# Loading the slot registers of the message sums one tile ahead of the row registers, on TensorE

## The chip, the core and the metric

The kernel runs on one core of a Trainium2 chip. The metric is the device time of one execution in microseconds, as the median of several runs. Engines are named as in the profile: PE is TensorE's matmuls, PEld its weight loads, DVE the vector engine, ACT the scalar engine, POOL is GpSimd, SP issues DMAs. A "q" behind an engine's name (PEldq) marks its sequencer, which runs register operations and waits.

## What is computed

The reference is a graph network of four layers, each followed by a residual and a layer norm. The change touches the fourth, an edge-conditioned convolution that repeats six steps over 212,500 edges of 12,500 nodes, with 32 features:

```python
eh = relu(e_feat @ en1_w.T + en1_b)
w_e = (eh @ en2_w.T + en2_b).reshape(-1, D, D)      # a 32 x 32 matrix for each edge
for _ in range(STEPS):                               # 6
    msg = einsum('ei,eio->eo', out[src], w_e)        # a message for each edge
    agg = segment_sum(msg, dst, num_segments=n_nodes) + conv_bias
    h = _gru_cell(relu(agg), h, ...)
    out = h
```

## The kernel before

Edges are sorted by destination. 128 edges are a tile, 16 tiles a group; a step has 104 groups (TG), and 110 (PG) groups of sums, since edges that don't fit spill into a tail. The edge matrices are not kept: each step computes them anew, tile by tile, in a loop on five engines whose turns two groups make (buffers s = 0 and 1).

For tile j of group g, the engines do this:
- GpSimd gathers the rows of the source nodes by an indirect DMA (line 1957), eight tiles ahead (LEAD), and multiplies the last 320 of 1024 products (`times`, line 1966).
- TensorE computes the 1024 entries of each edge's matrix (`matrices`, line 2066: two matmuls of 512 columns, four passes in the trace) into one of two buffers `p_w`. It first waits on `used`, which DVE raises when it has read the buffer two tiles earlier.
- ACT copies the 320 last entries out for GpSimd (`copy`, line 2010), and prepares the one-hot matrices `apart` for the sums.
- DVE multiplies the first 704 entries with the gathered rows (line 2147), then reduces the products of two tiles earlier (line 2136); for this it waits on `pooled`, GpSimd's part of that tile. Once per group it adds a finished sum (line 2118).
- TensorE sums messages by destination (`sum_up`, line 2082) with a small matmul. Where the sum goes (`row_regs`) and which slot of the ring of messages it reads (`slot_regs`) are registers: 16 of each, one per tile of the group.

The sums lag the matrices by eight tiles (LATER). Each turn j of `group` on TensorE issues the matrices of tile j and then one sum: for j below 8 one of the last eight sums of the group two back, from j = 8 on one of the first eight sums of the group before. At the first sum of a group `sum_up` loads both sets of registers from `slot_d` and `window_d` and then waits for the messages, for the one-hot matrices and for a cleared accumulator. All engines take their instructions in the order in which they are written; the order on TensorE is written out by hand.

Of the kernel before, what the change touches and what calls it, by code (L numbers as in the profile page):

```python
# [33 lines left out]
G = 16  # L34
# [7 lines left out]
TG = -(-E // (P * G))  # L42
# [15 lines left out]
def build(nc, a, out):  # L58
# [6 lines left out]
    class Phase(ExitStack):  # L65
# [6 lines left out]
        def sb(self, name, shape, dt=F32):  # L72
            return self.enter_context(nc.sbuf_tensor(f"{self.tag}_{name}", shape, dt))
# [37 lines left out]
    with top:  # L111
# [24 lines left out]
        with Phase('const') as ph:  # L136
# [3 lines left out]
            with nc.Block() as block:  # L140
                @block.sync
                def _(sp):
                    sp.dma_start(X[:, :], nodes(a["x"]).rearrange("l b f -> l (b f)")).then_inc(x_in, 16)
                    sp.dma_start(table[:, :], a["x"][:, :]).then_inc(x_in, 16)

                    sp.dma_start(wide_table[N:N + 1, :],
                                 a["zeros"][0:1, 0:2 * D]).then_inc(x_in, 16)
                    sp.wait_ge(x_in, 48)
                    sp.wait_ge(made, 4)
                    for i in range(4):  # L150
                        for j in range(4):
                            sp.dma_start(same_f[i * D:(i + 1) * D, j * D:(j + 1) * D],
                                         ident[0:D, 0:D]).then_inc(done, 16)
                    sp.wait_ge(done, 16 * 16)
# [398 lines left out]
        slot_regs = [nc.tensor.alloc_register(f"slot_at{j}") for j in range(G)]  # L553
        ring_regs = [nc.scalar.alloc_register(f"ring_at{s}") for s in range(2)]
        slot_d = sb("slot_d", [1, PAIRS], I32)
# [58 lines left out]
        with Phase("weights") as ph:  # L614
            zeroed, w_in = ph.sem("zeroed"), ph.sem("w_in")
            with nc.Block() as block:
                @block.vector
                def _(dve):
                    for t, _ in weights:
                        dve.memset(t[:, :], 0.0).then_inc(zeroed, 1)  # L620

                @block.sync
                def _(sp):
                    n = 0
                    for k, (_, parts) in enumerate(weights):
                        sp.wait_ge(zeroed, k + 1)
                        for to, of in parts:
                            with nc.allow_non_contiguous_dma(reason="bias columns"):
                                sp.dma_start(to, of).then_inc(w_in, 16)
                            n += 1  # L630
                    sp.wait_ge(w_in, 16 * n)
            ph.end()
# [1240 lines left out]
        with nc.Fori(0, STEPS) as step:  # L1873


            with Phase("l3m") as ph:
# [22 lines left out]
                LATE, LATER = 2, 8  # L1899
# [12 lines left out]
                with nc.Block() as block:  # L1912
# [146 lines left out]
                    @block.tensor  # L2059
                    def _(pe):  # L2060
                        def matrices(i, s, j):
                            t = (i * 2 + s) * G + j

                            pe.wait_ge(used, t + 1)
                            for c in range(2):
                                ins = pe.matmul(p_w[j % 2][:, c * 512:(c + 1) * 512], hid[s][:, j * P:(j + 1) * P],  # L2066
                                                en2[:, c * 512:(c + 1) * 512], start=True, stop=True)
                            ins.then_inc(mats, 1)

                        def sum_up(i, s, j, tail=False):  # L2070
                            g = i * 2 + s
                            if j == 0:
                                pe.load(slot_regs, slot_d[0:1, bass.ds(g * G, G)])
                                pe.load(row_regs, window_d[0:1, bass.ds(g * G, G)])
                                pe.wait_ge(found if tail else hits, g * 4 + 4)

                                pe.wait_ge(joined, (TG * PARTS if tail else g * PARTS + PARTS) + JOINED)

                                pe.wait_ge(cleared, g + 1)
                            at = pe.snap(row_regs[j], min_val=0, max_val=(G - 1) * D)  # L2080
                            of = pe.snap(slot_regs[j], min_val=0, max_val=(RB * G - 1) * D)
                            pe.matmul(p_sum[s][0:LO, bass.ds(at, D)], apart[s][:, j, :], slots[:, bass.ds(of, D)],  # L2082
                                      start=False, stop=True, skip_group_check=True).then_inc(summed, 1)

                        def group(i, s, older=True, newer=True):
                            pe.wait_ge(hid_in[s], i * 16 + 16)
                            for j in range(G):
                                matrices(i, s, j)
                                if j >= LATER:
                                    if newer:  # L2090
                                        sum_up(i + (s - 1), 1 - s, j - LATER)
                                elif older:
                                    sum_up(i - 1, s, G - LATER + j)

                        pe.sem_inc(summed, SUMMED)
                        pe.sem_inc(mats, MATS)
                        group(0, 0, older=False, newer=False)
                        group(0, 1, older=False)
                        with pe.Fori(1, TG // 2) as i:
                            group(i, 0)  # L2100
                            group(i, 1)
                        for j in range(G - LATER, G):
                            sum_up(TG // 2 - 1, 0, j)
                        for j in range(G):
                            sum_up(TG // 2 - 1, 1, j)
                        with pe.Fori(TG // 2, PG // 2) as i:
                            for s in range(2):
                                for j in range(G):
                                    sum_up(i, s, j, tail=True)
# [225 lines left out]
```

## Time and profile before

| | |
|---|---|
| time, median of 3 runs | 36760.22 us (36759.47 to 36788.16) |
| the profiled execution's own time | 36759.45 us |
| its span, from the first to the last instruction | 36757.7 us |
| PE busy | 27737.6 us (75%) |
| DVE busy | 25860.5 us (70%) |
| ACT busy | 12358.7 us (34%) |
| POOL busy | 28300.5 us (77%) |

The message loop fills the last 58% of the span, in six equal steps with a short stage for the node states between them. The shares are means over the whole span, and within the loop three engines are busy most of the time. What the loop waits for is therefore read from idle times and from the distance between equal instructions, not from shares.

### The profile page before, as it was taken

What the parts mean: (1) busy time and instruction counts of PE and PEld (TensorE: products, weight loads), DVE (VectorE), ACT (ScalarE), POOL (GpSimd) and SP (SyncE); (2) the same over time, 40 slices, a digit from 0 to 9 for tenths busy, and PEclk for the clock granted to TensorE, in tenths of its full rate; (3) what the DMA queues carried; (4) which work ended last, traced back from release to release, by engine and by line L of the source; (5) the groups of instructions that cost most, each with busy time, mean ns of one, the idle gap of its engine ahead of it and who ended that gap; (6) DMA issues with size and microseconds to landing.
All of it is one profiled execution on the core that took longest, in us unless ns stands there. A gap on an engine that the chain in (4) does not pass through costs nothing. (4 is left out here: it accounts for less than half of the span.)

```text
span 36757.7 us, 442832 instructions
## 1 busy us (share of the span) xinstructions
PE 27737.6 (75%) x91956; PEld 15930.9 (43%) x91957; DVE 25860.5 (70%) x34107; ACT 12358.7 (34%) x38546; POOL 28300.5 (77%) x30158
## 2 busy tenths in 40 slices
PE   6333346655583333499999999999999999999999
PEld 5000014445583333344444444444444444444444
DVE  8444432222451121399999999999999999999998
ACT  0000001111200000155555555555555555555554
POOL 1776777767507767699979997999799979988997
PEclk8555556655655555599999999999999999999999
DMA  0221012221310000111111111111111111111111
GB/s 19 48 47 29 23 39 82 81 33 27 84 41 14 14 14 14 23 49 49 49 45 49 49 49 45 49 49 49 45 49 49 49 45 49 49 45 48 49 49 44
DMA packets 1452401, 1590.59 MB, mean 43 GB/s; under 512 B 953756, under 2 KB 1115535, under 8 KB 1346959
## 3 DMA queue, kind: packets, MB, share of 16 engines
q1 hardware_dynamic: 743720, 1056.16, 9.1%
q0 software_dynamic: 645120, 473.02, 7.4%
q10 hardware_dynamic: 63360, 59.50, 0.6%
q14 instruction: 169, 1.38, 0.0%
q8 instruction: 32, 0.52, 0.0%
HBM read 1342.34 MB, written 246.33 MB: 43 GB/s over the span
## 5 line engine op out<-in xcount | busy, mean ns | idle before, releaser
L2066 PE MATMUL l3m_p_w<-en,l3m_hid 128*128 128x512 f32 x39936 | 19534.1, 617 | 177.2 <-DVE l3m_prod L2147 101.1
L2136 DVE TENSOR_REDUCE l3m_xg<-l3m_prod 128x32 f32<-128x1056 f32 x9984 | 12423.2, 1244 | 0.3
L1957 POOL DMA_INDIRECT l3m_xg<-wide_table,l3m_mt x9984 | 9783.8, 980 | 2452.9 <-issue 1549.9
L2147 DVE TENSOR_TENSOR l3m_prod<-l3m_p_w,l3m_xg 128x704 f32<-128x704 f32 x9984 | 8827.0, 884 | 542.0 <-ACT l3m_rest L2010 541.9
L1966 POOL TENSOR_TENSOR l3m_prod<-l3m_rest,l3m_xg 128x320 f32<-128x320 f32 x9984 | 8741.6, 876 | 366.6 <-ACT l3m_rest L2010 192.5
L2066 PEld LDWEIGHTS l3m_p_w<-en,l3m_hid 128*128 128x128 f32 x39936 | 6785.0, 189 | 5141.0 <-issue 4795.3
L2010 ACT COPY l3m_rest<-l3m_p_w 128x320 f32<-128x320 f32 x9984 | 4254.7, 426 | 9434.1 <-PE l3m_p_w L2066 8033.8
L2082 PEld LDWEIGHTS l3m_p_sum<-room,l3m_apart 128*125 128x125 f32 x21120 | 3936.3, 197 | 5586.1 <-issue 5586.1
L1996 ACT ACTIVATE l3m_apart<-iota_lo,l3m_lo 128x125 f32<-128x125 f32 x9984 | 3998.6, 401 | 0.0
L2082 PE MATMUL l3m_p_sum<-room,l3m_apart 128*125 x21120 | 3318.9, 246 | 644.6 <-issue 619.9
L893 POOL DMA_INDIRECT l2a_rows<-table,l2a_mt x1664 | 1575.9, 947 | 1619.3 <-DMA l2a_mt<-dst_meta 1112.6
L2020 ACT COPY l3m_prod<-l3m_xg 128x32 f32<-128x32 f32 x9984 | 2510.2, 251 | 0.0
L1254 POOL DMA_INDIRECT l1a_xg<-table,l1a_mt x1760 | 1684.9, 957 | 658.8 <-issue 658.8
L1010 POOL DMA_INDIRECT l_xg<-table,l_mt x1760 | 1674.1, 951 | 594.6 <-issue 536.0
L531 POOL DMA_INDIRECT by_dst<-order_src_rec,order_src_idx x1664 | 1631.2, 980 | 594.3 <-issue 505.8
L893 POOL DMA_INDIRECT l2b_rows<-table,l2b_mt x1664 | 1575.9, 947 | 657.0 <-issue 506.7
L531 POOL DMA_INDIRECT by_src<-order_dst_rec,order_dst_idx x1664 | 1627.6, 978 | 585.2 <-issue 506.9
L506 PE MATMUL order_dst_p_pos<-order_dst_count,band 101*128 101x512 f32 x832 | 823.7, 1140 | 1385.3 <-DVE order_dst_count L479 1385.3
L927 PE MATMUL l2a_p_acc<-l2a_rows,l2a_hit 128*125 x3520 | 759.6, 396 | 1450.0 <-SPq L860 1450.0
L927 PE MATMUL l2b_p_acc<-l2b_rows,l2b_hit 128*125 x3520 | 759.6, 396 | 1420.1 <-SPq L860 1420.1
L506 PE MATMUL order_src_p_pos<-order_src_count,band 101*128 101x512 f32 x832 | 823.7, 1141 | 1322.7 <-DVE order_src_count L479 1322.7
L2001 ACT ACTIVATE l3m_apart<-l3m_apart,ones 128x500 f32<-128x500 f32 x2496 | 1777.8, 712 | 81.2
(378 smaller groups left out, 19850.9 us busy)
## 6 DMA issues: line engine op xcount, KB each, us to landing
l3m_hid<-hid_t SPq DMA_DIRECT2D x624, 1024.0 KB
l3m_xg<-wide_table,l3m_mt POOLq DMA_INDIRECT x9984
hid_t<-l_hid SPq DMA_DIRECT2D x110, 1024.0 KB, 4.0
order_src_bk<-dst_bucket SPq DMA_DIRECT2D x52, 808.0 KB
order_dst_bk<-src_bucket SPq DMA_DIRECT2D x52, 808.0 KB
l_rec<-by_dst SPq DMA_DIRECT2D x110, 272.0 KB, 2.8
l_xg<-table,l_mt POOLq DMA_INDIRECT x1760
l1a_xg<-table,l1a_mt POOLq DMA_INDIRECT x1760, 2.4
```

The costliest lines, as they stand in the source:

```text
L531: pool.indirect_dma_start(rows, bass.IndirectOffsetOnAxis(ap=idx[s][:, t:t + 1], axis=0), rec[s][:, t, :], None).then_inc(sent[s], 16)
L893: pool.indirect_dma_start(rows[:, s * G + j, :], None, tab[:, :], bass.IndirectOffsetOnAxis(ap=mt[s][:, j, 0:1].bitcast(I32), axis=0)).the ...
L1957: pool.indirect_dma_start(xg[s][:, j, 0:2 * D], None, wide_table[:, :], bass.IndirectOffsetOnAxis(ap=mt[s][:, j, 0:1].bitcast(I32), axis=0 ...
L1966: pool.tensor_tensor(prod[j % RING][:, OWN:D, 0:D], o_i(rest[j % RING][:, :]), state_of(s, j, D - OWN), ALU.mult).then_inc(pooled, 1)
L1996: act.activation(apart[s][:, j, :], iota_lo[:, :], ACT.Abs, scale=-1.0, bias=lo[s][:, j:j + 1]).then_inc(distances, 1)
L2001: act.activation(quarter, quarter, ACT.Relu, scale=-1.0, bias=ones[:, 0:1]).then_inc(hits, 1)
L2010: act.copy(rest[j % RING][:, :], p_w[j % 2][:, OWN * D:HD]).then_inc(copied, 1)
L2020: act.copy(prod[j % RING][:, :, D:D + 1], xg[s][:, j, D:2 * D, None]).then_inc(biased, 1)
L2066: ins = pe.matmul(p_w[j % 2][:, c * 512:(c + 1) * 512], hid[s][:, j * P:(j + 1) * P], en2[:, c * 512:(c + 1) * 512], start=True, stop=True)
L2082: pe.matmul(p_sum[s][0:LO, bass.ds(at, D)], apart[s][:, j, :], slots[:, bass.ds(of, D)], start=False, stop=True, skip_group_check=True).th ...
L2136: dve.tensor_reduce(xg[s][:, j, 2 * D:3 * D], prod[j % RING][:, :, :], AX, ALU.add).then_inc(msgs, 1)
L2147: dve.tensor_tensor(prod[j % RING][:, 0:OWN, 0:D], o_i(p_w[j % 2][:, 0:OWN * D]), state_of(s, j, OWN), ALU.mult).then_inc(used, 1)
```

## The change

```diff
--- before.py
+++ after.py
@@ -2067,10 +2067,14 @@
                                                 en2[:, c * 512:(c + 1) * 512], start=True, stop=True)
                             ins.then_inc(mats, 1)
 
+                        def slots_of(g):
+                            pe.load(slot_regs, slot_d[0:1, bass.ds(g * G, G)])
+
                         def sum_up(i, s, j, tail=False):
                             g = i * 2 + s
                             if j == 0:
-                                pe.load(slot_regs, slot_d[0:1, bass.ds(g * G, G)])
+                                if tail:
+                                    slots_of(g)
                                 pe.load(row_regs, window_d[0:1, bass.ds(g * G, G)])
                                 pe.wait_ge(found if tail else hits, g * 4 + 4)
 
@@ -2091,6 +2095,9 @@
                                         sum_up(i + (s - 1), 1 - s, j - LATER)
                                 elif older:
                                     sum_up(i - 1, s, G - LATER + j)
+                                if newer and j == LATER - 1:
+
+                                    slots_of(i * 2 + (s - 1))
 
                         pe.sem_inc(summed, SUMMED)
                         pe.sem_inc(mats, MATS)
@@ -2101,6 +2108,7 @@
                             group(i, 1)
                         for j in range(G - LATER, G):
                             sum_up(TG // 2 - 1, 0, j)
+                        slots_of(TG - 1)
                         for j in range(G):
                             sum_up(TG // 2 - 1, 1, j)
                         with pe.Fori(TG // 2, PG // 2) as i:
```

The load of the slot registers leaves `sum_up` and becomes a function of its own. In the loop `group` calls it at j = 7, behind the last sum of the preceding group; the load of the row registers stays at the first sum, one tile later. After the loop it is called ahead of the last group's sums, and the groups of the tail (`tail=True`) load both as before. The rows below show TensorE's order in the loop, in the second half of the even group: from the last sum of one group (`p_sum0`) over `matrices` of tile 8 to the first sum of the next group (`p_sum1`). L2064 sets the value that a `matrices` waits for; ISA and REGISTER_ALU rows are register operations of the sequencer. Before:

```order
L2082 MATMUL l3m_p_sum0<-room,l3m_apart0 125x32
L2064 REGISTER_ALU
L2066 MATMUL l3m_p_w0<-en2,l3m_hid0 128x512 x2
L2073 ISA
L2073 TENSOR_LOAD slot_d
L2074 REGISTER_ALU
L2074 TENSOR_LOAD off_s
L2075 ISA
L2077 REGISTER_ALU
L2079 REGISTER_ALU
L2080 ISA
L2082 MATMUL l3m_p_sum1<-room,l3m_apart1 125x32
```

The same place after the change, where eight lines more in the file move the numbers (the sum is line 2086 now):

```order
L2086 MATMUL l3m_p_sum0<-room,l3m_apart0 125x32
L2071 ISA
L2071 TENSOR_LOAD slot_d
L2064 REGISTER_ALU
L2066 MATMUL l3m_p_w0<-en2,l3m_hid0 128x512 x2
L2078 ISA
L2078 TENSOR_LOAD off_s
L2079 ISA
L2081 REGISTER_ALU
L2083 REGISTER_ALU
L2084 ISA
L2086 MATMUL l3m_p_sum1<-room,l3m_apart1 125x32
```

The slots' load (`slot_d`) now stands ahead of the matmuls of tile 8 instead of behind them; the rows' load (`off_s`, the memory of `window_d`) stays between tile 8 and the first sum. The three register operations ahead of the sum's own (the waits for messages, one-hot matrices and accumulator) are the same in both. On the other engines the order is unchanged.

## Rows read from the trace of the kernel before

**Rows 1.** Costliest groups of the page: xcount | busy, mean ns | idle before, releaser

```profile
L2136 DVE TENSOR_REDUCE l3m_xg<-l3m_prod 128x32 f32<-128x1056 f32 x9984 | 12423.2, 1244 | 0.3
L1957 POOL DMA_INDIRECT l3m_xg<-wide_table,l3m_mt x9984 | 9783.8, 980 | 2452.9 <-issue 1549.9
L2147 DVE TENSOR_TENSOR l3m_prod<-l3m_p_w,l3m_xg 128x704 f32<-128x704 f32 x9984 | 8827.0, 884 | 542.0 <-ACT l3m_rest L2010 541.9
L1966 POOL TENSOR_TENSOR l3m_prod<-l3m_rest,l3m_xg 128x320 f32<-128x320 f32 x9984 | 8741.6, 876 | 366.6 <-ACT l3m_rest L2010 192.5
```

**Rows 2.** Waits in the message loop, 15440 to 36720: us in total, times, longest

```profile
PE l3m_p_sum L2082 <- issue: 619.9, 618, 1.1
```

**Rows 3.** Timeline of PE, tiles 7 to 9: start us, us, what [idle before]

```profile
20025.49 1.98 PE L2066 MATMUL l3m_p_w<-en,l3m_hid 128*128 128x512 f32 x4
20027.31 0.30 PE L2082 MATMUL l3m_p_sum<-room,l3m_apart 128*125 x2
20027.44 1.98 PE L2066 MATMUL l3m_p_w<-en,l3m_hid 128*128 128x512 f32 x4
20030.45 0.40 PE L2082 MATMUL l3m_p_sum<-room,l3m_apart 128*125 x2 [1.02 <-issue]
20030.68 1.96 PE L2066 MATMUL l3m_p_w<-en,l3m_hid 128*128 128x512 f32 x4
```

**Rows 4.** Lines of TensorE's sequencer there, last all: ns min/median/max, first to last start

```profile
L2080 PEldq FUSED_REGOPS  x1: 68/68/68, 20025.5 to 20025.5; - x1
...
L2064 PEldq ALU_OP  x1: 32/32/32, 20025.6 to 20025.6; - x1
...
L2073 PEldq TENSOR_LOAD <-slot_d x1: 1102/1102/1102, 20027.6 to 20027.6; - x1
...
L2074 PEldq TENSOR_LOAD <-off_s x1: 1103/1103/1103, 20028.9 to 20028.9; - x1
...
L2073 PEldq TENSOR_LOAD <-slot_d x660: 1102/1105/1115, 15496.9 to 36636.1; - x165
```

**Rows 5.** Timeline of DVE, the same group: products of tiles 7 to 9, an addition

```profile
20028.46 0.89 DVE L2147 TENSOR_TENSOR l3m_prod<-l3m_p_w,l3m_xg 128x704 f32<-128x704 f32 x1
...
20030.42 0.89 DVE L2147 TENSOR_TENSOR l3m_prod<-l3m_p_w,l3m_xg 128x704 f32<-128x704 f32 x1
...
20033.29 0.89 DVE L2147 TENSOR_TENSOR l3m_prod<-l3m_p_w,l3m_xg 128x704 f32<-128x704 f32 x1 [0.83 <-ACT l3m_rest L2010]
...
20036.06 0.68 DVE L2118 TENSOR_TENSOR acc_room<-acc_room,l3m_p_sum 125x512 f32 x1
```

**Rows 6.** Timeline of POOL, the same group: products of tiles 7 to 9

```profile
20028.98 0.87 POOL L1966 TENSOR_TENSOR l3m_prod<-l3m_rest,l3m_xg 128x320 f32<-128x320 f32 x1
...
20031.01 0.87 POOL L1966 TENSOR_TENSOR l3m_prod<-l3m_rest,l3m_xg 128x320 f32<-128x320 f32 x1
...
20033.34 0.86 POOL L1966 TENSOR_TENSOR l3m_prod<-l3m_rest,l3m_xg 128x320 f32<-128x320 f32 x1 [0.32 <-ACT l3m_rest L2010]
```

**Rows 7.** Line 1966 in two stretches of the second step, ten and eighty groups

```profile
L1966 POOL TENSOR_TENSOR l3m_prod<-l3m_rest,l3m_xg x161: 866/873/889, 19066.3 to 19391.5; 128x320 f32<-128x320 f32 x161
...
L1966 POOL TENSOR_TENSOR l3m_prod<-l3m_rest,l3m_xg x1280: 864/875/892, 19657.7 to 22281.9; 128x320 f32<-128x320 f32 x183
```

**Rows 8.** Timeline, second step, the products of its tile 32 on both engines

```profile
19062.32 0.88 DVE L2147 TENSOR_TENSOR l3m_prod<-l3m_p_w,l3m_xg 128x704 f32<-128x704 f32 x1
...
19066.33 0.88 POOL L1966 TENSOR_TENSOR l3m_prod<-l3m_rest,l3m_xg 128x320 f32<-128x320 f32 x1
```

**Rows 9.** Timeline, second step: POOL's tiles 0 and 1655, DVE's last product (1663)

```profile
19001.29 0.87 POOL L1966 TENSOR_TENSOR l3m_prod<-l3m_rest,l3m_xg 128x320 f32<-128x320 f32 x1
...
22392.57 0.87 POOL L1966 TENSOR_TENSOR l3m_prod<-l3m_rest,l3m_xg 128x320 f32<-128x320 f32 x1
...
22409.22 0.88 DVE L2147 TENSOR_TENSOR l3m_prod<-l3m_p_w,l3m_xg 128x704 f32<-128x704 f32 x1
```

**Rows 10.** Timeline of POOL, second step: two gathers, 88 tiles apart, with longer gaps

```profile
19575.24 0.97 POOL L1957 DMA_INDIRECT l3m_xg<-wide_table,l3m_mt  x1 [0.61 <-issue]
...
19755.35 0.97 POOL L1957 DMA_INDIRECT l3m_xg<-wide_table,l3m_mt  x1 [0.34 <-issue]
```

## The prediction

> **What bounds the kernel now.** I began with the costliest groups of the page [rows 1]. Four lines of the message loop (1957 to 2147), two on GpSimd (POOL) and two on DVE, lead the list beside TensorE's matmuls, and their counts give its shape: 9984 tiles, that is 624 groups of 16, 104 in each of six steps. Shares of busy time don't say who sets the pace here, so the next question is who stands still, and when. Two engines hardly do. DVE spends 884 + 1244 ns on a tile, the two overlapping a little, and was idle 542 us in all; GpSimd spends 876 + 980 ns and was kept waiting for ACT for 192.5 us in all. TensorE's sum is held up by "issue" 618 times for 619.9 us, about once a group and 1.0 us each time [rows 2].
>
> The timeline of TensorE shows that once [rows 3]. Four matmuls of tile 7 start at 20025.49, a sum at 20027.31, tile 8 at 20027.44; then the next sum comes at 20030.45, with 1.02 us of idle time before it, and tile 9 only at 20030.68. Without the hole the sum would follow 1.82 us after tile 8 (20027.31 less 20025.49) and tile 9 0.13 us later, at 20029.39. TensorE therefore loses 1.29 us per group. The sequencer's rows say why [rows 4]: two register loads of 1.10 us stand in that place, at 20027.6 and 20028.9, and nothing behind them is issued until the second is over at 20030.0. From there to the sum it is another 0.45 us of register work and waits.
>
> DVE feels the hole one tile later [rows 5]: its products start 1.96 us apart (20028.46, 20030.42), then 2.87 us apart, with 0.83 us idle until ACT's copy. In a group DVE has 16 x 1.96 + 0.68 us for adding the finished sum = 32.0 us of work of its own. GpSimd feels much less of it: between two of its products lie 2.33 us at that place, with 0.32 us idle [rows 6], and otherwise 2.03 us.
>
> The decisive view is one of GpSimd's products in two stretches of one step [rows 7]. Early in the step 161 of them take 19066.3 to 19391.5: 325.2/160 = 2.0325 us a tile, 32.52 us a group. Later 1280 take 19657.7 to 22281.9: 2624.2/1279 x 16 = 32.83 us a group. Why is the same loop faster early? After the start of a step GpSimd is behind: tile 32 begins on DVE at 19062.32 and on GpSimd at 19066.33 [rows 8], 4.0 us later. That backlog feeds it across the hole, and each group eats 32.83 - 32.52 = 0.31 us of it; after some 13 groups it is gone, and from then on the loop runs at the pace of DVE and TensorE, 32.0 + 0.83. So **two limits lie 0.31 us apart**: the hole in TensorE's stream, 32.83 us, and GpSimd's own work, 32.52 us.
>
> **The change, part by part.** Nothing is removed: TensorE still makes two loads per group. One moves. The load of the slots now stands after the last sum of the group before, ahead of tile 8; the load of the rows stays behind tile 8.
>
> The moved load. What does the sequencer do at that place now? The register operations of the last sum run at 20025.5, the wait value of tile 8 at 20025.6 [rows 4], and then it waits until DVE has freed the buffer; tile 8 starts at 20027.44 [rows 3]. That is about 1.77 us of nothing. A load with its address operation takes 1.3 us (20027.6 to 20028.9, from load to load). It would end near 20027.0, some 0.45 us before tile 8 can start, and costs nothing. The cover is the wait for DVE; if the sequencer came to this place more than 0.45 us later, the rest would show. The trace also shows that a load does not wait for the matmuls queued ahead of it: the first began 0.1 us after tile 8, whose four passes had 1.9 us to run. I take nothing, with 0 to 1.3 us as bounds.
>
> One rule speaks against the change. All 660 loads of the slots took 1.10 us for 16 registers [rows 4], 69 ns a register. The Trainium skill, "Runtime: NRT & Kernel Launch", section "Instruction fetch mechanics", puts such a load at about 200 ns a register even in bulk. By that rule, as an estimate, 16 registers would take 3.2 us, tile 8 would start about 1.5 us late and the sum still later, near 2.3 us per group or 38.2 ms in all. The trace does not agree, and the measured 1.10 us decides; I give the rule no chance.
>
> The load that stays. It begins at 20027.6, as the slots' load does now, and ends at 20028.7; with the same 0.45 us behind it the sum is ready to go at 20029.15. Tile 8's last pass lets it start at 20029.26. The hole closes; up to 0.1 us may be left, since the weight load of the sum comes late. Even a remainder of 0.5 us of the 0.83 us of DVE's idle time would not matter: DVE and TensorE then need 32.5 us a group, and GpSimd needs 32.52.
>
> What is late next. Once GpSimd is behind, DVE reduces a tile only when GpSimd has multiplied its part, so the backlog stays near the 4.0 us that the early stretch shows, and GpSimd has a product ready each time. The whole step runs like its first 13 groups. First and last product with a gather behind it lie at 19001.29 and 22392.57 [rows 9], 1655 tiles apart: 3391.3 us. At 2.0325 us a tile they take 3363.8. **Gain 27.5 us a step.**
>
> The end of a step. The last eight tiles have no gather, so GpSimd (0.87 us a product) catches up and DVE sets the end: today its last product starts 16.65 us after that product of GpSimd (22409.22) [rows 9]. With DVE 4.0 us ahead at that point, 8 x 1.96 + 0.68 - 4.0 = 12.4 us are left. **Gain 4.3 us a step.** The sums after the loop, the other loads and the first groups have both loads where they had them, or wait for DVE anyway: nothing.
>
> Sum: 6 x (27.5 + 4.3) = 191 us. The profiled execution took 36759.45 us, 0.8 below the median of the three runs; 36759.45 - 191 = 36568, and I say 36570.
>
> **The rivals.** *GpSimd pays for gaps that are hidden now.* Late in a step the gap before a gather, 0.16 us elsewhere, is 0.61 us once in 176 tiles [rows 10], and half-way between two of these 0.35 us. Today nobody waits for it, since GpSimd has time to spare. With GpSimd as the bound eight of each would cost 8 x (0.45 + 0.19) = 5.1 us a step, 31 us in all: 36600. For it: such a gap is GpSimd's own. Against it: none stands in the first 280 tiles of a step, when GpSimd is behind, though three places of the same spacing fall there; with work queued the gap seems to be covered.
>
> *The hole only shrinks.* If loads or waits leave 0.6 to 0.8 us of DVE's 0.83, the loop runs between 32.6 and 32.8 us and 624 groups give back 20 to 110 us: 36650 to 36740. Or the pace is held at 32.83 by something that the hole now conceals, such as the round trip of a product buffer through ACT and DVE: 36760. Against both: in every other tile DVE follows without idle time, and the early stretch shows 32.52 with the hole still there.
>
> *Slower: the moved load holds up tile 8.* Place: between the last sum and tile 8. If the sequencer only gets there when that sum has left TensorE (20027.4) and not at 20025.6, tile 8 starts 1.3 us late and the second load still leaves up to 0.3: 1.3 + 0.3 against the 1.29 of today, near 0.3 us a group, 624 x 0.3 = 187 us: 36945. It decides from the point at which the load begins more than 0.45 us later than the rows say. Against it: the register operations of the last sum run at 20025.5, long before the sum itself at 20027.31.
>
> **How the numbers follow.** Forecast 36570: 57%. Gaps of GpSimd paid: 23%. The hole only shrinks: 10%, of which 6% at no gain. Slower: 5%. The other 5% lie below the forecast or just above 36600. Range 36540 to 36650: it holds the first two cases with 30 us around them. A measurement of this kernel tells about 0.2% (74 us) from no change: faster by more than that 0.87, within it 0.08, slower 0.05.
>
> **What would show it.** In the changed kernel the sum behind tile 8 should have no idle time from issue (619.9 us now); the slots' load should start about 1.7 us before tile 8 and be over before it; DVE's idle time should sit at the reduction or its product and point to GpSimd; GpSimd's products should lie 2.03 us apart at every tile, with 32.5 us a group late in a step as early. The forecast is wrong if late groups still take 32.8 us, if tile 8 starts behind the moved load, or if GpSimd's own work per tile grows when it never rests.

## The result and the profile after

The changed kernel takes 36581.75 us (median of 5 runs, 36574.43 to 36585.35) against 36760.22 us for the kernel before (5 runs, 36758.87 to 36788.16): a ratio of 0.9949, with a 95% interval of 0.9935 to 0.9964. It is 178 us faster; 191 us were forecast, and the time lies 12 us above the forecast of 36570. The profiled execution is the median run, with a span of 36580.0 us.

The costliest groups of the page after, in the columns of [rows 1] (count, busy us and mean ns, idle us before and its releaser; ACT's copy and TensorE's sum are added):

```profile
L2144 DVE TENSOR_REDUCE l3m_xg<-l3m_prod 128x32 f32<-128x1056 f32 x9984 | 12466.9, 1249 | 0.4
L1957 POOL DMA_INDIRECT l3m_xg<-wide_table,l3m_mt x9984 | 9778.5, 979 | 2427.8 <-issue 1592.4
L1966 POOL TENSOR_TENSOR l3m_prod<-l3m_rest,l3m_xg 128x320 f32<-128x320 f32 x9984 | 8754.9, 877 | 201.3 <-ACT l3m_rest L2010 25.3
L2155 DVE TENSOR_TENSOR l3m_prod<-l3m_p_w,l3m_xg 128x704 f32<-128x704 f32 x9984 | 8812.2, 883 | 38.7 <-ACT l3m_rest L2010 38.4
L2010 ACT COPY l3m_rest<-l3m_p_w 128x320 f32<-128x320 f32 x9984 | 4247.1, 425 | 9261.0 <-PE l3m_p_w L2066 9255.7
L2086 PE MATMUL l3m_p_sum<-room,l3m_apart 128*125 x21120 | 3266.5, 244 | 24.7 <-ACT room L2026 24.7
```

DVE's product waited 541.9 us for ACT and now waits 38.4; GpSimd's wait for ACT fell from 192.5 to 25.3 us. The sum of TensorE no longer names "issue" (619.9 us in [rows 2]).

The timeline of TensorE over tiles 6 to 8 of one group, as [rows 3] (start us, duration us, what; an idle time would stand in brackets):

```profile
20024.24 1.98 PE L2066 MATMUL l3m_p_w<-en,l3m_hid 128*128 128x512 f32 x4
20026.06 0.30 PE L2086 MATMUL l3m_p_sum<-room,l3m_apart 128*125 x2
20026.28 1.98 PE L2066 MATMUL l3m_p_w<-en,l3m_hid 128*128 128x512 f32 x4
20028.10 0.31 PE L2086 MATMUL l3m_p_sum<-room,l3m_apart 128*125 x2
20028.30 1.98 PE L2066 MATMUL l3m_p_w<-en,l3m_hid 128*128 128x512 f32 x4
```

The tile at 20026.28 is tile 8 and the one at 20024.24 tile 7. The first sum starts 1.82 us after tile 8, as behind any other tile, with no idle time. The lines of TensorE's sequencer in the same stretch, as [rows 4] (ns, first to last start), tell why:

```profile
L2071 PEldq TENSOR_LOAD <-slot_d x1: 1105/1105/1105, 20024.5 to 20024.5; - x1
...
L2064 PEldq ALU_OP  x1: 32/32/32, 20025.7 to 20025.7; - x1
...
L2078 PEldq TENSOR_LOAD <-off_s x1: 1104/1104/1104, 20026.4 to 20026.4; - x1
```

The slots' load starts 1.8 us before tile 8, is over at 20025.6, and the wait value of tile 8 is set at 20025.7, about 0.6 us before the tile starts. The rows' load lies under tile 8.

GpSimd's product in an early and a late stretch of the second step, ten and eighty groups, as [rows 7] (ns min/median/max, first to last start):

```profile
L1966 POOL TENSOR_TENSOR l3m_prod<-l3m_rest,l3m_xg x161: 867/877/891, 19041.0 to 19366.4; 128x320 f32<-128x320 f32 x161
...
L1966 POOL TENSOR_TENSOR l3m_prod<-l3m_rest,l3m_xg x1281: 867/876/892, 19626.7 to 22229.5; 128x320 f32<-128x320 f32 x183
```

The early stretch takes 325.4/160 x 16 = 32.54 us a group, the late one 2602.8/1280 x 16 = 32.535 us. The difference that before showed between them, 32.52 and 32.83 us, is gone. The timelines of the two engines in that step, as [rows 8] and [rows 9], show the lag between them and the step's end:

```profile
18975.98 0.87 POOL L1966 TENSOR_TENSOR l3m_prod<-l3m_rest,l3m_xg 128x320 f32<-128x320 f32 x1
...
22225.63 0.88 DVE L2155 TENSOR_TENSOR l3m_prod<-l3m_p_w,l3m_xg 128x704 f32<-128x704 f32 x1
...
22229.51 0.88 POOL L1966 TENSOR_TENSOR l3m_prod<-l3m_rest,l3m_xg 128x320 f32<-128x320 f32 x1
...
22341.34 0.89 POOL L1966 TENSOR_TENSOR l3m_prod<-l3m_rest,l3m_xg 128x320 f32<-128x320 f32 x1
...
22353.82 0.88 DVE L2155 TENSOR_TENSOR l3m_prod<-l3m_p_w,l3m_xg 128x704 f32<-128x704 f32 x1
```

Tile 1600 of the step starts on GpSimd 3.88 us after DVE: the lag that tile 32 had before (4.0 us) now lasts through the step. From GpSimd's tile 0 to its tile 1655 it takes 22341.34 - 18975.98 = 3365.4 us (before 3391.3), and DVE's last product follows 12.48 us later (before 16.65). That is 25.9 + 4.2 = 30.1 us a step, 181 us in six. The loop itself began 5.4 us later in this execution than in the profiled one of before (its first product on GpSimd at 15459.6 against 15454.2), in stages that the change doesn't touch.

### The profile page after: what moved, and what is told of

Its sections match the earlier page's. It is cut to its first block and busy times, and to the rows that moved or that the text cites. A ratio compares the mean times of both kernels' runs of the same rounds, so it can differ in the third digit from the quotient of the medians.

```text
span 36580.0 us, 442832 instructions
## 1 busy us (share of the span) xinstructions
PE 28012.3 (77%) x91956; PEld 16265.6 (44%) x91957; DVE 26185.1 (72%) x34107; ACT 12349.5 (34%) x38546; POOL 28310.3 (77%) x30158
## 5 line engine op out<-in xcount | busy, mean ns | idle before, releaser
L1966 POOL TENSOR_TENSOR l3m_prod<-l3m_rest,l3m_xg 128x320 f32<-128x320 f32 x9984 | 8754.9, 877 | 201.3 <-ACT l3m_rest L2010 25.3
L2155 DVE TENSOR_TENSOR l3m_prod<-l3m_p_w,l3m_xg 128x704 f32<-128x704 f32 x9984 | 8812.2, 883 | 38.7 <-ACT l3m_rest L2010 38.4
L2010 ACT COPY l3m_rest<-l3m_p_w 128x320 f32<-128x320 f32 x9984 | 4247.1, 425 | 9261.0 <-PE l3m_p_w L2066 9255.7
```

The costliest lines, as they stand in the source:

```text
L1966: pool.tensor_tensor(prod[j % RING][:, OWN:D, 0:D], o_i(rest[j % RING][:, :]), state_of(s, j, D - OWN), ALU.mult).then_inc(pooled, 1)
L2010: act.copy(rest[j % RING][:, :], p_w[j % 2][:, OWN * D:HD]).then_inc(copied, 1)
L2155: dve.tensor_tensor(prod[j % RING][:, 0:OWN, 0:D], o_i(p_w[j % 2][:, 0:OWN * D]), state_of(s, j, OWN), ALU.mult).then_inc(used, 1)
```

## The experiments

The theory: after the change GpSimd's own work (32.5 us a group) is the bound, and TensorE's hole counts only as far as it takes DVE beyond that. The rivals: what is left of the hole, or the load that stays in it, still sets the pace; or a round trip of buffers does, in which GpSimd's share has no part. Lines move by a few in each kernel, so line 2086 of after is 2087, 2089 or 2083 in some of them.

**Half of the slots behind tile 8 again.** From the changed kernel; eight of the sixteen slot registers are loaded early and eight at the old place, so that part of the hole comes back:

```diff
-                        def slots_of(g):
-                            pe.load(slot_regs, slot_d[0:1, bass.ds(g * G, G)])
+                        def slots_of(g, a=0, n=G // 2):
+                            pe.load(slot_regs[a:a + n], slot_d[0:1, bass.ds(g * G + a, n)])
...
+                                slots_of(g, G // 2)
                                 pe.load(row_regs, window_d[0:1, bass.ds(g * G, G)])
```

> Half of the slots' load is back at the old place: 8 registers ahead of tile 8, the other 8 and the 16 rows behind it. Theory (GpSimd sets the pace at 32.53 us a group; DVE and TensorE need 32.0 us plus what of TensorE's hole reaches DVE): a load of 8 registers takes 0.6 to 0.8 us, the sum behind tile 8 comes some 0.75 us late, DVE would lose about 0.3 us a group and need 32.3, still under 32.53. So the time stays that of the changed kernel, 36582 within 30 us, with the hole visible on TensorE and no gain of GpSimd lost. Rival (a hole in TensorE's stream costs what it takes away, there is no second limit): between the two kernels or worse, 0.3 x 624 = 180 us more, 36760.

Measured: 36575.84 us (36573.66 to 36583.86). Its timeline of TensorE at tile 8, and its waits over the whole loop (us in total, times, longest):

```profile
20020.99 1.98 PE L2066 MATMUL l3m_p_w<-en,l3m_hid 128*128 128x512 f32 x4
20023.59 0.40 PE L2087 MATMUL l3m_p_sum<-room,l3m_apart 128*125 x2 [0.62 <-issue]
```

```profile
PE l3m_p_sum L2087 <- issue: 325.4, 612, 0.6
...
DVE l3m_prod L2156 <- ACT l3m_rest L2010: 95.7, 319, 6.7
```

The hole is there, about half the waiting of before (325.4 us against 619.9), and DVE feels it in about half of the groups. The time doesn't: it is that of the changed kernel. A hole of this size is not paid.

**Both loads ahead of tile 8.** From the changed kernel, the other way round: 2.2 us of loads are put where the sequencer has 1.77 us to spare.

```diff
                         def slots_of(g):
                             pe.load(slot_regs, slot_d[0:1, bass.ds(g * G, G)])
+                            pe.load(row_regs, window_d[0:1, bass.ds(g * G, G)])
...
-                                pe.load(row_regs, window_d[0:1, bass.ds(g * G, G)])
```

> Both loads stand ahead of tile 8, none behind it. Theory: the cover ahead of tile 8 is one tile's wait, about 1.8 us, and two loads with their operations take 2.6, so tile 8 starts 0.7 to 0.9 us late in every group and the sum behind it has no hole; DVE loses about 0.4 us a group and needs 32.4, GpSimd still sets the pace: 36582 to 36610. Rival one (the cover is longer than a tile, loads ahead of tile 8 are free): no idle time of TensorE from issue at tile 8, 36582. Rival two (the hole costs what it takes away wherever it stands): near the kernel before, 36760.

Measured: 36576.39 us (36574.07 to 36580.08). Timeline of TensorE, tiles 7 and 8, and the waits:

```profile
20018.99 1.98 PE L2066 MATMUL l3m_p_w<-en,l3m_hid 128*128 128x512 f32 x4
20020.81 0.30 PE L2086 MATMUL l3m_p_sum<-room,l3m_apart 128*125 x2
20021.77 1.98 PE L2066 MATMUL l3m_p_w<-en,l3m_hid 128*128 128x512 f32 x4 [0.66 <-issue]
```

```profile
PE l3m_p_w L2066 <- issue: 411.5, 618, 0.7
DVE l3m_prod L2155 <- ACT l3m_rest L2010: 185.6, 624, 6.8
```

The cover that the prediction spoke of is real and has an end: two loads of 1.3 us with their address work are 2.6 us, 0.83 more than the 1.77 that are spare, and tile 8 starts 2.78 us after tile 7 instead of 1.95, 0.66 us of it shown as idle. DVE stands 185.6/624 = 0.30 us a group, and even so the time is the same, since DVE then needs 32.0 + 0.3 us and GpSimd 32.5.

**One tile in four: a column from GpSimd to DVE.** From the changed kernel; in every fourth tile DVE takes 23 of the 32 columns instead of 22, and ACT's copy and GpSimd's product shrink accordingly (32 of 320 elements):

```diff
+                def own(j):
+                    return OWN + (j % 4 == 3)
...
-                            pool.tensor_tensor(prod[j % RING][:, OWN:D, 0:D], o_i(rest[j % RING][:, :]),
-                                               state_of(s, j, D - OWN), ALU.mult).then_inc(pooled, 1)
+                            pool.tensor_tensor(prod[j % RING][:, own(j):D, 0:D], o_i(rest[j % RING][:, 0:HD - own(j) * D]),
+                                               state_of(s, j, D - own(j)), ALU.mult).then_inc(pooled, 1)
...
```

> The changed kernel, with one more of the 32 columns of products given from GpSimd to DVE in every fourth tile (23 instead of 22). Theory (GpSimd is the bound): GpSimd saves about 0.08 us in four tiles of a group, 32.53 - 0.33 = 32.2; DVE gets 4 x 0.033 = 0.13 more, 32.0 to 32.15. The group takes 32.2 us, 624 x 0.33 = 206 us less: 36376, at least 36450. Rival (DVE and TensorE still set the pace): slower by 0.13 x 624 = 82 us, 36664.

The same shift was made in the kernel before:

> The kernel before, with the same shift of one column in every fourth tile. Theory (before the change the hole makes DVE and TensorE the bound at 32.83 us): DVE gets 0.13 us a group more, so it is slower by about 624 x 0.13 = 82 us, 36842; GpSimd waits more. Rival (GpSimd was the bound before as well, or both share the pace): faster, by up to 206 us, 36554 to 36760.

Measured: in the changed kernel 36402.28 us (36400.45 to 36405.24), 179 us below it, where 206 were expected. In the kernel before 36818.66 us (11 runs) against 36761.83 (15 runs beside it), a ratio of 1.0015 (1.0006 to 1.0024): 57 us slower, where 82 were expected. GpSimd's product over eighty groups of the second step in the two kernels, the changed one first:

```profile
L1969 POOL TENSOR_TENSOR l3m_prod<-l3m_rest,l3m_xg x1281: 797/873/892, 19589.0 to 22169.7; 128x320 f32<-128x320 f32 x137, 128x288 f32<-128x288 f32 x46
```

```profile
L1969 POOL TENSOR_TENSOR l3m_prod<-l3m_rest,l3m_xg x1281: 797/871/892, 19666.1 to 22300.2; 128x320 f32<-128x320 f32 x137, 128x288 f32<-128x288 f32 x46
```

The first makes 2580.7/1280 x 16 = 32.26 us a group, 0.28 less than 32.535: four columns at 0.07 us, all of it gained. The second makes 2634.1/1280 x 16 = 32.93 us, 0.10 more than 32.83. A column more lengthens DVE's product from 885 to 917 ns there, so four cost it 0.13 us a group; three of the four come out as time, and the one at the hole only shortens the wait there (2.83 us from product to product across the hole instead of 2.86, the mean of eighty groups). So before the change GpSimd's work had no say late in a step, and after it it has all of it. One edit with opposite signs in the two kernels is the strongest sign here that the bound has moved.

**The other direction.** From the changed kernel, GpSimd gets one column more in every tile:

```diff
-                OWN = 22
+                OWN = 21
```

> The changed kernel with one column of products more on GpSimd in every tile (DVE 21 of 32 instead of 22). Theory (GpSimd is the bound): the run with a column less in a quarter of the tiles gave 32.53 to 32.26 us a group, 0.07 us a column, so 16 columns more add 1.1 us: 33.65 us a group, 624 x 1.1 = 690 us, 37270. Rival (DVE and TensorE set the pace): DVE has 16 x 0.025 = 0.4 us a group less, so not slower than 36582.

Measured: 37249.4 us (37236.3 to 37256.35), a ratio of 1.0134 to the kernel before. GpSimd's product there:

```profile
L1966 POOL TENSOR_TENSOR l3m_prod<-l3m_rest,l3m_xg x1281: 934/944/961, 19751.7 to 22442.2; 128x352 f32<-128x352 f32 x183
```

That is 33.63 us a group, 1.10 more, for a product that takes 944 ns instead of 876 (0.068 x 16 = 1.09). GpSimd's work is paid in full. These shifts change ACT's copy as well, but ACT isn't the bound: in the changed kernel it stands idle 9261.0 us ahead of its 9984 copies, 0.93 us each on average, and a column changes its copy by 0.03 us (452 ns here instead of 425), not by the 0.07 us that a column is worth.

**No load behind tile 8 at all.** From the changed kernel; both sets are loaded in halves of eight registers behind the sums of tiles 3, 6, 10 and 13, each ahead of a tile for whose buffer the sequencer waits anyway (`load_half` loads eight registers from the given place on):

```diff
...
-                                if newer and j == LATER - 1:
-
-                                    slots_of(i * 2 + (s - 1))
+                                if newer and j in HALVES:
+                                    load_half(*HALVES[j][:2], i * 2 + (s - 1), HALVES[j][2])
...
+                        HALVES = {3: (slot_regs, slot_d, 0), 6: (row_regs, window_d, 0),
+                                  10: (slot_regs, slot_d, G // 2), 13: (row_regs, window_d, G // 2)}
...
```

Registers in use by the eight sums that are still to come are left alone: the first halves are replaced at tiles 3 and 6, the second at 10 and 13.

> No load is left between tile 8 and the sum behind it: both sets are loaded in halves of 8 registers, behind tiles 3, 6, 10 and 13, where the old values are used up. Theory: the load that the change leaves in place is hidden already, and GpSimd sets the pace, so the time is that of the changed kernel, 36570 to 36590, GpSimd at 32.53 us a group. Rival (the load that stays still costs some 0.1 us a group): 36520.

Measured: 36574.96 us (36568.69 to 36580.3). GpSimd's product there:

```profile
L1966 POOL TENSOR_TENSOR l3m_prod<-l3m_rest,l3m_xg x1281: 865/876/893, 19623.6 to 22226.6; 128x320 f32<-128x320 f32 x183
```

32.54 us a group again. The load that the change leaves behind tile 8 costs nothing, and the four kernels with no hole or a small one (the changed one, and the three experiments on its loads) agree within 7 us.

**Three loads in the hole.** From the kernel before, the slots' load written twice, to price a load at the place where it is paid:

```diff
                                 pe.load(slot_regs, slot_d[0:1, bass.ds(g * G, G)])
+                                if not tail:
+                                    pe.load(slot_regs, slot_d[0:1, bass.ds(g * G, G)])
```

> The kernel before with a third register load at the old place (the slots are loaded twice). Theory: DVE and TensorE are the bound there, and a load more lengthens the hole by its 1.1 us and its operations: TensorE loses about 1.25 us more, all of it reaches DVE, 34.1 us a group, 624 x 1.25 = 780 us: 37540. Rival (a load costs only what the two before left over, or the sequencer runs ahead of it): 36762 to 37000.

Measured: 36754.62 us against 36753.33 beside it, a ratio of 1.0 (0.9991 to 1.0009). This run tells nothing on the price: the sequencer's rows have the slots' load once per group, at the second of the two lines, so the repeated one was not in the program that ran.

```profile
L2075 PEldq TENSOR_LOAD <-slot_d x660: 1102/1105/1115, 15493.1 to 36630.0; - x165
```

**The slots in four loads.** The same question put so that no load repeats another: from the kernel before, four loads of four registers at the old place.

```diff
-                                pe.load(slot_regs, slot_d[0:1, bass.ds(g * G, G)])
+                                for a in range(0, G, G // 4):
+                                    pe.load(slot_regs[a:a + G // 4], slot_d[0:1, bass.ds(g * G + a, G // 4)])
```

> The kernel before, with the slots' load at its old place cut into four loads of 4 registers. The run with half a load showed 0.59 us for 8 registers against 1.10 for 16, so a load of 4 takes about 0.34 us and each more load 0.18 us of register operations: 4 x 0.34 + 3 x 0.18 = 1.9 us in place of 1.1. Theory (the hole of TensorE is the bound before the change, and what lengthens it is paid in full): 0.8 us more a group, 33.6 us, 624 x 0.8 = 500 us, 37250. Rival (the hole is partly hidden, so that a longer one costs a part): 36750 to 37000.

Measured: 37591.87 us (37567.73 to 37609.61) against 36789.3 beside it, 1.022 (1.0203 to 1.0237): 803 us more, where some 500 were expected. The timeline of TensorE at two neighbouring groups, then stretches at the first of them (length, busy us and count of PE, PEld, DVE, ACT and POOL, granted clock of TensorE, DMA share, GB/s):

```profile
20026.42 1.98 PE L2066 MATMUL l3m_p_w<-en,l3m_hid 128*128 128x512 f32 x4
20030.17 0.40 PE L2083 MATMUL l3m_p_sum<-room,l3m_apart 128*125 x2 [1.76 <-ACT room L2026]
20030.40 3.08 PE L2066 MATMUL l3m_p_w<-en,l3m_hid 128*128 128x512 f32 x4
...
20065.36 0.40 PE L2083 MATMUL l3m_p_sum<-room,l3m_apart 128*125 x2 [1.70 <-ACT room L2026]
20065.59 1.96 PE L2066 MATMUL l3m_p_w<-en,l3m_hid 128*128 128x512 f32 x4
```

```profile
20028.50:20030.00 1.50, 0.00 (x0) 0.00 (x0) 1.50 (x2) 1.03 (x4) 1.32 (x3) 1.00 0.13 22
20030.00:20031.00 1.00, 0.83 (x4) 0.60 (x5) 1.00 (x2) 0.00 (x0) 0.84 (x2) 1.00 0.16 33
20031.00:20034.00 3.00, 3.00 (x7) 1.50 (x6) 0.44 (x1) 0.33 (x2) 0.97 (x1) 0.52 0.09 14
```

The hole is 1.76 and 1.70 us instead of 1.02. (The trace names "ACT room" there, a copy that was over at 20029.6; the loads ran until 20029.7.) At the second group that is all: tile 9 takes its 1.96 us. At the first one the granted clock falls to 0.52 behind the hole, the lower of its two levels (1.2 of 2.4 GHz), tile 9 takes 3.08 us, and DVE then idles 2.69 us. By the distance of DVE's products from one group to the next, 404 of 618 groups take 33.47 us on average (33.52 in the median), close to the 33.6 expected, and the other 214 take 35.23 us. In the kernel before, the same mean is 32.80 us: 404 x (33.47 - 32.80) + 214 x (35.23 - 32.80) = 271 + 520 = 791 us, nearly all of the 803. The longer hole accounts for 618 x 0.67 = 414 us of it, which is paid practically in full (0.67 us a group, the first groups of each step with their backlog included, for a hole longer by 0.68 to 0.74 us), and the lower clock behind it for 214 x 1.76 = 377 us. In the kernel before, with 1.02 us of idle time, the granted clock was 1.00 over the eighty late groups of [rows 7].

**A version that goes on.** Since the two engines' limits can now be set against each other, the shift was taken to where they should meet: six tiles in sixteen.

```diff
+                def own(j):
+                    return OWN + (j % 8 in (1, 4, 6))
...
```

`own(j)` takes the place of `OWN` in GpSimd's product, ACT's copy and DVE's product, as with one tile in four.

> The changed kernel with one more column on DVE in six of sixteen tiles (four gave 36402). Theory: GpSimd gets 32.53 - 6 x 0.07 = 32.11 us a group, DVE needs 32.0 + 6 x 0.025 = 32.15 at most: the two meet, the group takes 32.11 to 32.15 us, 36402 less 624 x 0.11 to 0.15: 36310 to 36335. Rival (DVE or TensorE has become the bound by four already): 36402 or slower.

Measured: 36317.71 us (36314.08 to 36320.79), 0.9881 of the kernel before (0.9866 to 0.9896): the best of all the kernels here, 264 us below the changed one. GpSimd's product and, from its timeline, DVE's stream:

```profile
L1969 POOL TENSOR_TENSOR l3m_prod<-l3m_rest,l3m_xg x1281: 797/871/892, 19571.9 to 22141.2; 128x320 f32<-128x320 f32 x115, 128x288 f32<-128x288 f32 x68
```

```profile
20024.14 0.89 DVE L2158 TENSOR_TENSOR l3m_prod<-l3m_p_w,l3m_xg 128x704 f32<-128x704 f32 x1
20024.94 1.25 DVE L2147 TENSOR_REDUCE l3m_xg<-l3m_prod 128x32 f32<-128x1056 f32 x1
20026.10 0.92 DVE L2158 TENSOR_TENSOR l3m_prod<-l3m_p_w,l3m_xg 128x736 f32<-128x736 f32 x1
```

A group takes 2569.3/1280 x 16 = 32.12 us. DVE's products are 1.96 us apart, its own pace. The means over eighty groups are 1.957 us, 1.990 behind a tile with a column more and 2.555 across the addition, so its work is 9 x 1.957 + 6 x 1.990 + 2.555 = 32.11 us; GpSimd's is 32.535 - 6 x 0.07 = 32.115. Both engines are full.

Last, this shift together with the loads spread as in the experiment with halves:

> Six of sixteen tiles with one more column on DVE, and no load between tile 8 and its sum (halves behind tiles 3, 6, 10 and 13). Theory: with six, DVE runs without a break and is the bound together with GpSimd; TensorE's loads are hidden in either form, so 36318 within 20 us. Rival (a rest of the hole behind tile 8 reaches DVE now that it has no slack): faster, up to 60 us.

Measured: 36385.6 us (36381.01 to 36393.56), on another chip, where the kernel before took 36789.3 and not 36753.33 us; against that one it is 0.9891 (0.9875 to 0.9908), which can't be told from 0.9881. GpSimd's product there:

```profile
L1969 POOL TENSOR_TENSOR l3m_prod<-l3m_rest,l3m_xg x1281: 800/872/894, 19605.8 to 22180.2; 128x320 f32<-128x320 f32 x115, 128x288 f32<-128x288 f32 x68
```

That is 32.18 us a group, 0.06 more than in the run before: GpSimd's gathers take 982 ns on average where they took 979, and its products 852 ns where they took 850, which makes 0.07 us over 16 tiles. Over 624 groups 0.06 us are 37 us, and the loop started 26 us later in this execution, in stages without these loads: together 63 of the 68 us between the two times. GpSimd's own work sets the pace, so no hidden remainder of the hole was left to take; why its instructions are longer in this run is open.

## Why the prediction was right

**The hole.** Its working held. The load lies in the sequencer's wait, 1.8 us before tile 8 (about 1.7 foretold), and the sum has no idle time from issue any more. The remainder "up to 0.1 us" that the prediction left for the weight load of the sum is not there: the sum starts 1.82 us behind tile 8.

**Two limits 0.31 us apart.** This is the step that carried the number, and it is shown: GpSimd's late pace is its early one, its lag stays at 3.88 us through the step, its own work is paid to the full when it grows (33.63 us) and gained when it shrinks (32.26 us), and the shift that gains after the change loses before it. This second limit is also what kept the change from giving more: of DVE's 0.83 us of idle time a group only 0.3 us came out as time, and DVE spends the rest waiting for GpSimd. The prediction's sum for the pace before, 32.0 + 0.83 = 32.83 us, meets the measured 32.83 by luck, with two errors of 0.1 that cancel. DVE's own work is 16 x 1.957 + 0.60 = 31.9 us: an addition takes 0.68 us but sets the products back by only 0.60 (shown below). And the hole costs DVE 2.87 - 1.96 = 0.91 us, more than the 0.83 counted as idle. The forecast takes the two paces from GpSimd's rows, so its 27.5 us a step do not hang on this.

**The sum.** The tiles of a step were to take 3363.8 us and take 3365.4; the end of the step 12.4 us, measured 12.48. The mis-sized term is GpSimd's group, 32.52 us in the prediction and 32.535 in the run: 0.015 x 624 = 9 us, nearly all of the 10 us between 191 and 181. Between the two profiled executions lie 177.7 us: the later start of the loop, 5.4 us, is no part of the change and takes the 181 to 176, and the last 2 us are within the spread of the runs. GpSimd's product takes 877 ns and not 876 on average; why is open.

**The rivals.** *Gaps of GpSimd paid* (36600): the time, 36582, lies between this rival and the forecast and doesn't tell them apart, but the trace does: the gaps vanished. The longest idle time before a gather in the loop's waits is now 0.3 us, where [rows 10] had 0.61:

```profile
POOL l3m_xg L1957 <- issue: 1592.4, 9971, 0.3
```

*The hole only shrinks*: it closed. *The moved load holds up tile 8*: it was over before tile 8 was due; the experiment with both loads ahead shows the mechanism at twice the size, and even there it didn't reach the time.

**One tell-tale failed.** DVE was to show idle time at its reduction or product, pointing to GpSimd. The groups show 0.4 and 38.7 us. The timelines of both engines show where the waiting is, DVE's first:

```profile
20023.30 0.88 DVE L2155 TENSOR_TENSOR l3m_prod<-l3m_p_w,l3m_xg 128x704 f32<-128x704 f32 x1
20024.17 1.25 DVE L2144 TENSOR_REDUCE l3m_xg<-l3m_prod 128x32 f32<-128x1056 f32 x1
...
20033.46 0.88 DVE L2155 TENSOR_TENSOR l3m_prod<-l3m_p_w,l3m_xg 128x704 f32<-128x704 f32 x1
20034.26 0.68 DVE L2126 TENSOR_TENSOR acc_room<-acc_room,l3m_p_sum 125x512 f32 x1
...
20036.02 0.88 DVE L2155 TENSOR_TENSOR l3m_prod<-l3m_p_w,l3m_xg 128x704 f32<-128x704 f32 x1
20036.81 1.24 DVE L2144 TENSOR_REDUCE l3m_xg<-l3m_prod 128x32 f32<-128x1056 f32 x1
```

```profile
20023.26 0.87 POOL L1966 TENSOR_TENSOR l3m_prod<-l3m_rest,l3m_xg 128x320 f32<-128x320 f32 x1
```

The first reduction starts 0.04 us after GpSimd's product ends (20024.13), 0.87 us behind the start of DVE's own product. Behind the addition, where DVE doesn't wait, that is 0.79 us (20036.02 to 20036.81). So DVE does wait for GpSimd, 0.07 us in such a tile, but its instructions overlap and the profile counts no gap. It doesn't wait in every tile: the addition sets it back 0.6 us (20033.46 to 20036.02 is 2.56 us, not 1.96), and for some seven tiles it catches up at its own pace before it waits again. The 0.6 us between its own work, 31.9 us, and GpSimd's 32.5 are spread over about half of the 16 tiles and appear nowhere as idle time. From 19657 to 22284 us the profile counts DVE as busy for 2627.0 of 2627.0 us, and GpSimd, which sets the pace, for 2398.5.

## What to carry to other kernels

A stretch in which one engine has a backlog shows the limit that comes next, before the change is made: compare the distance of equal instructions there with that in the steady state, and cap the gain at the difference. Work that an in-order sequencer must do is free where it waits for a semaphore anyway, as long as it ends before that wait does; measure that spare time before filling it. When a hole is closed and the bound moves to another engine, a division of work that suited the old bound need not suit the new one: here a new one brought 264 us, more than the change itself, where the same kind of shift had made the kernel before slower.

## What the runs showed that was not expected

- **The clock of TensorE fell behind a longer hole, but not behind each.** With some 1.7 us of idle time once a group, the granted clock fell to its lower level in about a third of the groups, and such a group took 1.76 us more than the others. With 1.02 us of idle time, in the kernel before, it stayed at 1.00 over the eighty late groups of a step. The holes with a fall and those without are equally long (1.74 and 1.73 us on average), so what decides between them is open.
- **The price of a register load** on TensorE's sequencer goes with its registers: 1.10 us for sixteen and, in the rows of the two experiments with smaller loads, 0.59 us for eight and 0.33 us for four, so about 0.07 us for the load and 0.065 for each register.

```profile
L2071 PEldq TENSOR_LOAD <-slot_d x2: 588/591/594, 20019.2 to 20021.2; - x2
```

```profile
L2074 PEldq TENSOR_LOAD <-slot_d x4: 332/333/337, 20026.6 to 20028.1; - x4
```

- **GpSimd's gaps of 0.6 us** before every 176th gather are gone in every kernel in which GpSimd has work queued (the longest is 0.3 us in the changed kernel, in the one with OWN = 21 and in the one with six tiles in sixteen), and are there again, 0.6 us, in the one with the slots in four loads, where it waits. What they are is not shown.
